# A two-layer conditioned transformer stage in fp32: six first maxima, the exp table, two DMA orders and one wait moved across the border between the QKV stage and attention

## What is computed

```python
emb = silu(t) @ ada_w + ada_b                      # six rows of shifts, scales, gates
x = x + gate_msa * (gelu(mod(ln(x)) @ ssm_w1 + b) @ ssm_w2 + b)
x = x + gate_mlp * (gelu(mod(ln(x)) @ ff_w1 + b) @ ff_w2 + b)
h = sln(x, w)                                      # gamma * layernorm + beta
q, k, v = split(h @ Wqkv.T + bqkv)                 # 16 heads of 32
att = softmax(q @ k.T) / 512 ** 0.5
h1 = (att @ v) @ Wp.T + bp + x
y = sln(h1, w) + h1
```

## Time and profile before

| | us |
|---|---|
| median of 3 executions | 1861.26 |
| each of them | 1860.9, 1867.59, 1861.26 |
| profiled execution, its time | 1867.83 |
| profiled execution, its span | 1865.7 |
| PE, DVE, POOL, ACT busy | 1815.0, 1252.1, 1217.5, 836.4 |
| granted PE clock, mean | 0.989 of full |
| last QKV product of V ends | 898.05 |
| first attention matmul | 903.52 |
| last attention matmul, about | 1756 |

### The profile page before, as it was taken

One profiled execution on the slowest core, in us unless ns is written; L12 is line 12 of the kernel. 1 busy time (PEld: TensorE's weight loads), 2 busy tenths in 40 slices (PEclk: granted clock), 3 DMA queues, 4 the chain that ended last, 5 costly groups with the idle time before them and its releaser, 6 DMA issues. The chain is left out here.

```text
span 1865.7 us, 27084 instructions
## 1 busy us (share of the span) xinstructions
PE 1815.0 (97%) x9510; PEld 1214.0 (65%) x9510; DVE 1252.1 (67%) x1986; ACT 836.4 (45%) x1547; POOL 1217.5 (65%) x681
## 2 busy tenths in 40 slices
PE   8999999999999999999999999999999999999897
PEld 4678888888888788888555545554555555454376
DVE  4655655655655565556887777777777777777387
ACT  3223123122223122221476666666666666666465
POOL 2665465465464243332588888888988888898565
PEclk9999999999999999999999999999999999999999
DMA  7410110210103657595877778777878787865796
GB/s 271 118 35 23 57 34 22 56 34 22 56 1 118 209 206 244 180 292 181 199 164 175 184 167 184 175 181 177 182 179 185 172 182 170 185 153 133 232 383 235
DMA packets 135373, 287.10 MB, mean 154 GB/s; under 512 B 23984, under 2 KB 41520, under 8 KB 127200
## 3 DMA queue, kind: packets, MB, share of 16 engines
q1 hardware_dynamic: 102996, 200.10, 35.8%
q0 software_dynamic: 9264, 66.11, 17.4%
q10 hardware_dynamic: 23008, 19.54, 3.3%
HBM read 134.68 MB, written 84.19 MB: 117 GB/s over the span
## 5 line engine op out<-in xcount | busy, mean ns | idle before, releaser
L1619 DVE TENSOR_REDUCE at_mrow<-banks 128x1 f32<-128x512 f32 x976 | 594.1, 681 | 163.7 <-PE banks L1465 163.6
L1715 POOL TENSOR_TENSOR at_sums<-at_probs 128x2048 f32<-128x2048 f32 x127 | 596.6, 4698 | 91.5 <-DMA at_sums<-at_sums 80.2
L1599 ACT ACTIVATE at_probs<-banks 128x512 f32<-128x512 f32 x1024 | 519.7, 621 | 182.7 <-PE banks L1483 177.4
L1465 PE MATMUL banks<-early_ks,early_qs 96*128 96x512 f32 x976 | 407.9, 418 | 11.0 <-DVE at_mrow L1619 7.1
L1483 PE MATMUL banks<-early_qs,early_ks 98*128 98x512 f32 x1024 | 408.0, 417 | 1.8 <-ACT at_probs L1599 1.8
L1465 PEld LDWEIGHTS banks<-early_ks,early_qs 96*128 96x128 f32 x976 | 184.8, 189 | 145.1 <-DVE at_mrow L1619 91.6
L1483 PEld LDWEIGHTS banks<-early_qs,early_ks 98*128 98x128 f32 x1024 | 193.7, 190 | 105.6 <-ACT at_probs L1599 81.5
L1495 PE MATMUL banks<-at_probs,at_v 128*32 128x512 f32 x2048 | 249.1, 603 | 0.7 <-DMA at_v<-v_scratch 0.7
L66 PE MATMUL banks<-l_nt,l_weights 128*128 128x512 f32 x768 | 179.4, 394 | 5.4 <-DVEq L1193 4.3
L66 PE MATMUL banks<-l_ht,l_weights 128*128 128x512 f32 x768 | 178.9, 393 | 1.9 <-issue 1.9
L657 ACT ACTIVATE l_gt<-banks,mod 128x512 f32<-128x512 f32 x60 | 45.1, 778 | 299.3 <-PE banks L526 263.5
(11 more groups left out here) (147 smaller groups left out, 2155.3 us busy)
## 6 DMA issues: line engine op xcount, KB each, us to landing
at_sums<-at_sums POOLq DMA_DIRECT2D x63, 1024.0 KB, 8.3
qk_scratch<-qk_out SPq DMA_DIRECT2D x64, 512.0 KB, 6.1
early_ks<-qk_scratch SPq DMA_DIRECT2D x48, 512.0 KB, 5.2
early_qs<-qk_scratch SPq DMA_DIRECT2D x96, 256.0 KB, 5.7
attn_scratch<-at_out SPq DMA_DIRECT2D x32, 512.0 KB, 7.5
o_a<-attn_scratch SPq DMA_DIRECT2D x32, 512.0 KB, 14.5
chunk_in<-x SPq DMA_DIRECT2D x8, 1024.0 KB, 5.4
v_scratch<-qk_v ACTq DMA_DIRECT2D x32, 256.0 KB, 3.0
```

The source lines that it names most:

```text
L1465: pe.matmul(em[n % 3][:], qs[0:96, slot, half, j, c * P:(c + 1) * P], ks[0:96, slot, j, keys * CH:(keys + 1) * CH], start=True, stop=True) ...
L1599: nc.scalar.activation(probs[:, i % 4, j, :], et[n % 3][:], ACT.Exp).then_inc(exp_done, 1)
L1619: nc.vector.tensor_reduce(mrow[:, half, keys, u:u + 1], em[n % 3][:], AX.X, ALU.max).then_inc(max_done, 1)
L1715: nc.gpsimd.tensor_tensor(into, probs[:, a], probs[:, a + 1], ALU.add).then_inc(pair_ready, 1)
```

## The change

FIRST_MAXIMA goes from 48 to 42, so the six maxima after V leave the QKV stage. Group 0 takes them in attention: pairs 0 and 1 now have 11 products each in place of 8, and the three that FRONT has no place for come after the pair's `av`. In the place of the six, PE waits for V's first tile to be read and does four matmuls of 512 columns into bank 4 whose result nobody uses. ACT runs a one-column Exp before the last V store, which loads the exp table there. ACT no longer waits at the end of QKV for the V stores to land; SP waits for them in attention, before it loads the V of group 2. SP issues the six query loads of group 1 before the copies of negated maxima and not after. The load of `wp_raw` moves on ACT from the start of attention to behind step 8 of group 0. The last hunk makes the semaphore `v_free` outlive the stage.

```diff
--- before.py
+++ after.py
@@ -24,7 +24,7 @@
 A_RING = 4
 UNITS = HG * TT
 LEAD = 6
-FIRST_MAXIMA = 8 * LEAD
+FIRST_MAXIMA = 8 * LEAD - 6
 
 L0_EPS, L1_EPS = 1e-6, 1e-5
 F32 = mybir.dt.float32
@@ -916,6 +916,7 @@
             return ctx.enter_context(nc.semaphore(name))
 
         NM = 2 * KT
+        WARM = 4
 
         w = sh.w0[:, :, 0:3].rearrange("p a c (k n) -> p a c k n", k=KT)
         x = [sh.xa, sb("qk_x", [P, TT, D])]
@@ -930,6 +931,7 @@
         mv = sb("qk_mv", [P, TT, 2])
         ve = sb("qk_ve", [P, TT])
         rstd = sb("qk_rstd", [P, TT])
+        exp_warm = sb("qk_exp_warm", [P, 1])
 
         x_loaded = [sem("qk_x_loaded0"), sem("qk_x_loaded1")]
         stats_ready, mv_ready = sem("qk_stats_ready"), sem("qk_mv_ready")
@@ -943,7 +945,7 @@
         bv_loaded = sem("qk_bv_loaded")
         bp_added, x_stored = sem("qk_bp_added"), sem("qk_x_stored")
         v_done, v_ready = sem("qk_v_done"), sem("qk_v_ready")
-        v_free = sem("qk_v_free")
+        v_free = sh.v_free
 
         ps = sh.ps
         x_v = sh.x2_d.rearrange("(s t p) d -> s p t d", s=NCH, p=P)
@@ -989,12 +991,12 @@
 
             sp.wait_ge(qk_done, NM * NCH)
             load_stack_keys(sp, sh, sh.early_ks, 1, 0)
+            for half in range(QH):
+                load_stack_queries(sp, sh, sh.early_qs, 1, 0, half)
             sp.wait_ge(sh.negt_taken, 1)
             for part in range(2):
                 dst = sh.early_qs[96 + part:97 + part, RING - 1, 0].bitcast(F32).rearrange("o j (c q) -> o (j c) q", q=P)
                 sp.dma_start(dst, sh.neg_t[:, part]).then_inc(sh.negm_loaded, 16)
-            for half in range(QH):
-                load_stack_queries(sp, sh, sh.early_qs, 1, 0, half)
             sp.wait_ge(qk_free, 16 * NM * (NCH + 1))
             sp.wait_ge(x_stored, 16 * NCH)
             sp.wait_ge(sh.stack_loaded[RING - 1], 16 * STACK_LOADS)
@@ -1063,8 +1065,10 @@
                     if last and t == TT - 2:
                         turn_first(s)
                 if last:
-                    for n in maxima:
-                        maximum(s, n)
+
+                    pe.wait_ge(v_ready, TT * s + 1)
+                    for _ in range(WARM):
+                        pe.matmul(ps[KT][:], w[:, HI, 2, 0, 0:P], w[:, HI, 2, 0, :], start=True, stop=True)
 
             pe.sem_inc(turned, TT)
             step(0, 0, False)
@@ -1105,6 +1109,8 @@
                                   v[:, t, :].rearrange("p (g f) -> p g f", g=KT)).then_inc(v_free, 16)
 
                 for t in range(TT):
+                    if b_next is None and t == TT - 1:
+                        nc.scalar.activation(exp_warm[:], sh.eps[:, 0, 0:1], ACT.Exp)
                     store(t)
 
             act.dma_start(bp[:], sh.biasrows_in[R_BP].partition_broadcast(P)).then_inc(bv_loaded, 16)
@@ -1115,7 +1121,6 @@
                 step(2 * b + 1, b, b + 1, 1)
                 step(2 * b + 2, b + 1, b + 1, 0)
             step(NCH - 1, B - 1, None, 1)
-            act.wait_ge(v_free, 16 * TT * (NCH + 1))
 
         @block.vector
         def _(dve):
@@ -1178,10 +1183,6 @@
                     nc.vector.tensor_tensor(v[:, t, :], ps[KT + t][:], bv[:], ALU.add).then_inc(v_ready, 1)
                     if loads is None and t == TT - 2:
                         negate_first()
-                if loads is None:
-                    for n in maxima:
-                        take_maximum(n)
-
 
             nc.vector.memset(ve[:], 0.0).then_inc(qk_free, 16 * NM)
             nc.vector.memset(rstd[:], 0.0).then_inc(v_free, 16 * TT)
@@ -1331,7 +1332,12 @@
                 return []
             whose, at = (g + 1, (slot + 1) % RING) if p >= SWITCH else (g, slot)
             n = 4 * ((p - SWITCH) % PAIRS)
-            return [(whose, at, (n + a) // UNITS, (n + a) % UNITS, keys) for a in range(4) for keys in range(2)]
+            products = [(whose, at, (n + a) // UNITS, (n + a) % UNITS, keys) for a in range(4) for keys in range(2)]
+            if g == 0 and p < SWITCH:
+
+                rest = [(g, slot, *first_max(n)) for n in range(FIRST_MAXIMA, 4 * UNITS)]
+                products = rest[:len(rest) // 2] if p == 0 else rest[len(rest) // 2:]
+            return products
 
         def number(g, half, u, keys):
 
@@ -1356,6 +1362,9 @@
                     load_stack_queries(sp, sh, qs, g, slot, 0, (1, 2))
                     load_stack_queries(sp, sh, qs, g, slot, 1)
                 if part == 3:
+                    if g == 2:
+
+                        sp.wait_ge(sh.v_free, 16 * TT * (NCH + 1))
                     load_v(g, slot)
 
             def load_projection(g, part):
@@ -1549,6 +1558,8 @@
                         turn_max(g + 1, 0)
                     av(g, slot, 2 * p)
                     av(g, slot, 2 * p + 1)
+                    for product in products:
+                        max_unit(*product)
                     if p % 2 == 1:
                         den_before(g, p)
 
@@ -1597,6 +1608,8 @@
                         n = HG * (STEPS * g + i) + j
                         act.wait_ge(et_done, n + 1)
                         nc.scalar.activation(probs[:, i % 4, j, :], et[n % 3][:], ACT.Exp).then_inc(exp_done, 1)
+                    if first and i == KC:
+                        act.dma_start(wp_raw[:], wp_t.rearrange("(k p) n -> p k n", p=P)).then_inc(wp_loaded, 16)
                     if g == 1 and i % KC in (3, 5):
                         split_wp(2 * (i // KC) + (i % KC - 3) // 2)
                     if i % KC == KC - 1:
@@ -1607,7 +1620,6 @@
                         take_den(g, 0)
 
 
-            act.dma_start(wp_raw[:], wp_t.rearrange("(k p) n -> p k n", p=P)).then_inc(wp_loaded, 16)
             groups(act, group)
             take_den(G - 1, 1)
 
@@ -1939,6 +1951,7 @@
         sh.zeros = sb("zeros", [P, D], F32R)
         sh.minus_half = sb("minus_half", [P, TT])
         sh.eps = sb("eps", [P, 2, TT])
+        sh.v_free = ctx.enter_context(nc.semaphore("qk_v_free"))
         sh.e_done, sh.max_done, sh.mrow_turned, sh.maxima_joined, sh.negt_hi, sh.negt_taken, sh.negm_loaded = (
             ctx.enter_context(nc.semaphore("at_" + name))
             for name in ("e_done", "max_done", "mrow_turned", "maxima_joined", "negt_hi", "negt_taken", "negm_loaded"))
```

## The result

The change makes the kernel a little slower: 1869.93 us median of 8 executions against 1863.31 for the kernel before, run beside it (also 8). The ratio over all executions is 1.0034, with a 95% interval from 1.0024 to 1.0044, so the change costs 6.3 us (4.5 to 8.2). The profiled execution took 1874.88 us.

A forecast was written before the change was run, and what follows sets the result against it. PE, busy in 97% of the span, was taken to bound the kernel. Border -1.7, six maxima +3.66 and wp_raw +1.5 gave +3.5 us on the median 1861.26, so 1864.8 us; range 1857 to 1871.5.

The forecast's parts named there:

- The three terms of the sum: Border gain -1.7 us, extra maxima before fronts 1 and 2 +3.66, wait for quad 1 in `den` +1.5; together +3.5.
- The two clusters: Executions of the kernel before: two at 1861, and an upper cluster 6.6 us above the median, with the run of 1867.59.
- The border: QKV to attention: barrier opens early, copies hold the first M until 902.5, V products start at 908.7; gain 1.7 us.
- six queries behind the keys take 6.7 us: SP's queue at the border: the last query load lands 6.7 us after the third key load, at 902.3.
- a copy lands with the last load ahead of it: SP's queue: the small copies of negated maxima land at about 902.4, the last query at 902.3.
- the prediction's bounds: Border gain at most 5.9 us; a loss of 0.5 if the two last V stores go ahead of the copies.
- The six maxima: Three extra products before each of fronts 1 and 2, at DVE's pace: 1.83 us each, 3.66 in all.
- The rival of cheap maxima: Fronts 1 and 2: extra maxima cost only PE's own 1.7 us in place of 3.66; 1862.9 us, chance 0.14.
- wp_raw: Group 0, pair 5: the moved load slows quad 1, so `den` waits about 1.5 us; bounds 0 and 3.0.
- the first rival: Border: copies land in time and the clock stays up; -0.7 us in sum, 1860.5 us, chance 0.24.
- The slower loop: Later groups: each of PE's 51 quad waits grows; at 0.3 us each +15.3, 1880 us; chance 0.08.

## Why the prediction was right, and where it was off

**Direction and size.** Forecast was +3.5 us, 1864.8, with the range to 1871.5. Measured was +6.3 (4.5 to 8.2) and 1869.93, in the upper part of the range. The direction was right, but it was called too small to be measured, and eight executions of each kernel measure it: the interval leaves 1 out. The three terms of the sum were -1.7, +3.66 and +1.5. The traces have 0.0, +3.6 and +2.5. Of the 5.1 us between 1864.8 and 1869.93 another 2.0 are the base, a median of three executions: of eight it is 1863.31. The two clusters that the forecast saw in those three are not there in eight, which lie spread from 1860.9 to 1868.7.

**The border, mis-sized by 1.7 us.** The mechanism was right: the barrier opens early, and the copies then hold the first M, landing 5.7 us after issue behind the queries. Two sizes were off. The step "six queries behind the keys take 6.7 us" measured 7.2: the last was issued at about 891.9 and landed 13.6 us later, at 905.5, +4.7. And the step that a copy lands with the last load ahead of it measured 0.7 more. One possible reason for the 7.2 stands among the prediction's bounds: V stores of 256 KB were under way beside the queries, of which the one issued at 899.08 took 7.1 us to land. No run isolates their share. The first M came 1.1 us later than forecast. The other 0.6 is the front. I took 6.2 us for it, measured when the clock was already down for 2 us; here it fell half a microsecond ahead of the first M and stayed down for the whole front, 6.8 us.

**The six maxima, right.** 1.80 and 1.77 us against 1.83 each, three reductions at DVE's pace. The rival of cheap maxima falls. That price is the one behind `av`, which is where the change puts them; between the two `av` of a pair it was 1.05 us a pair. What the prediction did not see is that with this order of SP's queue the same six cost nothing where they stood: the run with 48 has the same first M. The sum credits the change with an earlier barrier, and the barrier was not what PE waited for.

**wp_raw, right in place and short in sum.** `den` of pair 5 lost 1.4 us where 1.5 were forecast; undoing the move gives back 2.6. The missing 1.1 is what follows from a late `den`, which the sum had left out: 0.7 us because the 8 KB copy of its result now lands behind query loads when DVE waits for it, 0.4 in the step after it, of which 0.19 is a wait for quad 2.

**The Trainium skill's ceiling.** By the Trainium skill's 435 GB/s (DMA: Bandwidth & Descriptors, Specifications) the copies would have been in time. The figure is a ceiling for all traffic, and the trace does not contradict it: the windows from 898 to 906 have 266 to 342 GB/s in all, the next one 418. What fails is to take it as the rate of these loads. 1.57 MB of queries in 7.2 us is 218 GB/s, and the first rival falls with it.

**Not foreseen.** The prediction treated SP's reordering as a cost only. Undoing it (copies first) does not free the border, because SP's 3.1 us of issuing and V behind the queries take its place.

**The slower loop** is not seen beyond the one disturbed quad: PE's idle time for quads is 37.0 us in the changed kernel's profile and 31.1 before. The twelve other kernels have 23.7 to 34.7, so 37.0 is the highest, and one profile cannot say whether that is the change. It did not cost time after pair 8, where the changed execution was 1.8 us faster than the one before.

## What to carry to other kernels

When a wait is removed at a barrier, list what the first instruction behind it waits for, with landing times: here all of 3.7 us at the barrier went into one 8 KB copy issued behind 1.5 MB, and a second 8 KB copy, behind a late `den`, cost 0.7 more. Work that fills such a wait is free, and moving it to a place where an engine paces it costs its full price. A large transfer that has no due time is best kept away from every transfer that has one: 1 MB beside quad 1 cost 2.5 us here. The border gained 6.4 us only where the query loads stood out of the way of both the barrier and the small copies, and then V of group 1 was late for pair 2.

## What the runs showed of the hardware

- Issuing is work on the path: six query loads took SP 2.9 to 5.0 us, and in the run with the copies first the barrier opened 0.85 us after the last of them.
- 32-column products of two heads take as long as those of four before a full-width matmul can follow (0.98 and 1.00 us). One full-width matmul behind every two heads cost 0.94 us, three in one block between two steps 0.35 each; 0.23 to 0.34 is its pace in a front.
- An 8 KB copy landed 1.9 us after issue on an empty queue, and 5.5 to 6.2 us behind loads or stores of 256 KB.
- A load of 1 MB issued 0.8 us ahead of a 1 MB accumulating DMA goes with 10.2 us for the latter, and 7.0 where the load stood elsewhere. The four other runs with the load in that place have 9.9 to 10.2.
- In the changed kernel and in the one without dummies the clock fell at +5.0 and +4.9, so four matmuls in the pause made no difference to it.
